# The shift of the entry layer norm in a Mamba and local attention kernel: five small ScalarE instructions in place of one VectorE product of two SBUF operands

## The reference

```
x = x + layernorm(mamba(layernorm(x)))
x = x + layernorm(attention_stack(layernorm(x)))
```

## Time and profile before

| | us |
|---|---|
| median of 3 runs | 2461.28 |
| lowest and highest | 2460.6, 2464.99 |
| the profiled execution, its own time | 2461.61 |
| its span, first to last instruction | 2459.8 |
| mean granted TensorE clock | 0.943 |
| TensorE, VectorE, ScalarE, GpSimd busy | 1893.9, 1892.7, 1778.1, 1711.4 |

### The profile page before, as it was taken

How to read it: one execution, slowest core, us unless ns; L and a number is a source line. 1 busy time by engine, 2 the same in 40 slices (tenths; PEclk the granted TensorE clock), 3 DMA queues, 4 the chain that set the end, 5 groups by cost and what they waited for, 6 DMA issues and landing times.

```text
span 2459.8 us, 44075 instructions
## 1 busy us (share of the span) xinstructions
PE 1893.9 (77%) x15808; PEld 1114.3 (45%) x15936; DVE 1892.7 (77%) x3477; ACT 1778.1 (72%) x3955; POOL 1711.4 (70%) x1540
## 2 busy tenths in 40 slices
PE   2156778797878879797878879697888879787865
PEld 0013345353635445363635445363645545363634
DVE  3557797978879797988878797988879797887442
ACT  2245778696978878696878878696877869685644
POOL 1969595977959596886959596885959597792010
PEclk9977999899999989999999999999999989999988
DMA  4444443535344343534544353534543353531000
GB/s 162 126 120 115 112 105 104 132 83 146 103 130 117 100 121 92 134 86 131 129 129 103 103 124 96 138 87 130 130 115 99 110 127 90 137 99 33 17 20 9
DMA packets 126346, 261.09 MB, mean 106 GB/s; under 512 B 26928, under 2 KB 59696, under 8 KB 125872
## 3 DMA queue, kind: packets, MB, share of 16 engines
q1 hardware_dynamic: 126128, 258.27, 39.6%
HBM read 185.42 MB, written 42.99 MB: 93 GB/s over the span
## 4 chain that ended last, share of the span: by engine, by line
PE 38%; DVE 23%; ACT 13%; issue 9%; POOL 8%; DMA 4%; SPq 0%; DVEq 0%; POOLq 0%; ACTq 0%
DVE hs L618 6%; DVE m L892 4%; PE f_bank L342 4%; PE b_bank L342 4%; DVE kr L906 3%; POOL gy L663 3%; DMA spread<-steps 3%; POOL dbu L646 3%; ACT da L594 3%; PE b_bank L703 3%; PE f_bank L746 3%; PE y_sum L571 2%; DVE b_bank L896 2%; PE b_bank L773 2%; DVE ss L879 2%
## 5 line engine op out<-in xcount | busy, mean ns | idle before, releaser
L618 DVE TENSOR_TENSOR_SCAN hs<-da,dbu 128x512 f32<-128x512 f32 x512 | 622.2, 1215 | 127.1 <-POOL dbu L646 82.0
L663 POOL TENSOR_TENSOR gy<-hs,bc 128x512 f32<-128x512 f32 x512 | 652.1, 1274 | 41.5 <-DVE hs L618 31.2
L646 POOL TENSOR_TENSOR dbu<-spread,bc 128x512 f32<-128x512 f32 x512 | 651.5, 1274 | 9.1 <-DMA spread<-steps 9.0
L594 ACT ACTIVATE da<-spread,rest 128x512 f32<-128x512 f32 x512 | 359.4, 702 | 159.0 <-DVE hs L618 135.1
L703 PE MATMUL b_bank<-rest,h_t 128*128 128x512 f32 x384 | 227.9, 694 | 96.6 <-DVE kr L906 92.5
L960 POOL TENSOR_TENSOR kr<-kr,rn 128x512 f32<-128x512 f32 x256 | 264.8, 1043 | 42.3 <-ACT rn L817 37.0
L703 PE MATMUL f_bank<-rest,h_t 128*128 128x512 f32 x384 | 217.6, 665 | 72.1 <-DVE kr L906 64.2
L571 PE MATMUL y_sum<-gy,rest 128*32 128x512 f32 x1024 | 147.0, 649 | 92.4 <-POOL gy L663 92.3
L342 PE MATMUL f_bank<-first,kr 128*128 128x128 f32 x768 | 128.4, 298 | 78.9 <-DVE kr L906 49.8
L342 PE MATMUL b_bank<-first,kr 128*128 128x128 f32 x768 | 123.7, 296 | 57.8 <-DVE kr L906 41.8
L1106 POOL TENSOR_TENSOR xs<-xs,v 128x512 f32<-128x512 f32 x16 | 18.9, 1183 | 213.3 <-ACT xs L337 213.3
(11 more groups left out here) (168 smaller groups left out, 4748.2 us busy)
## 6 DMA issues: line engine op xcount, KB each, us to landing
spread<-steps SPq DMA_DIRECT2D x256, 512.0 KB, 5.1
vs<-v SPq DMA_DIRECT2D x96, 260.0 KB, 5.9
bc<-bc_rows SPq DMA_DIRECT2D x32, 512.0 KB, 6.2
steps<-k_t SPq DMA_DIRECT2D x32, 512.0 KB, 2.7
gate<-gates SPq DMA_DIRECT2D x32, 512.0 KB, 5.7
gates<-kr SPq DMA_DIRECT2D x16, 512.0 KB, 3.4
gates<-late SPq DMA_DIRECT2D x16, 512.0 KB, 4.3
vs<-v SPq DMA_DIRECT2D x32, 130.0 KB, 4.5
```

Of the source, the lines that this page charges most:

```text
L594: e.activation(da[:, :], spread[:, slot(b, s // 2), 0, :], ACT.Exp, scale=a_neg[:, s:s + 1]).then_inc(decayed.sem, 1)
L618: e.tensor_tensor_scan(hs[:, s % 2, :], da[:, :], dbu[:, s % 2, :], 0.0, ALU.mult, ALU.add).then_inc(scanned.sem, 1)
L646: e.tensor_tensor(dbu[:, s % 2, :], spread[:, slot(b, s // 2), 1, :], bc[:, s % 2, :], ALU.mult).then_inc(fed.sem, 1)
L663: e.tensor_tensor(gy[:, s % 8, :], hs[:, s % 2, :], bc[:, 2 + s % 2, :], ALU.mult).then_inc(read_out.sem, 1)
```

## The change

Four things change.

1. In the entry, VectorE no longer makes the shift. `dve_enter` loses that step.
2. ScalarE makes it instead, in one new step, `act_norm_shift`: a copy of the means with scale -1 into `lv` (128x4), and then four products of 128x1 elements, `lv[:, t] * rs[:, t]`, with `rs` as the scale operand. It waits on itself before the products (`negated`) and before the normalisation (`shifted`). The other layer norms keep L331.
3. Two counters are added, and `n_e` counts two measurements in place of three. `act_normalise` no longer waits for VectorE in the entry.
4. The table `ORDER` is written anew for all engines. Most of it stands as it was. Steps change places with their neighbours in many spots, and at SP some move further.

```diff
 ORDER = {
     "pe": (
-        "A1 B1 A1 B1 A1 B3 A3 B2 A3 B5 A1 B1 A1 B2 A2 B3 A1 B1 A1 M1 B2 A2 B1 M1 A1 B1 A1 B4 A1 B1 A1 B4 A1 B4 A1 "
+        "A1 B1 A1 B1 A2 B1 A1 B2 A1 B2 A1 B2 A1 B1 A1 B2 A2 B2 A1 B3 A1 B1 A1 M1 B1 A1 B2 A2 B1 A1 M1 B1 A1 B4 A1 "
...
     "sp": (
-        "M1 F2 M5 A1 M1 B1 M1 E1 B1 M3 A1 M6 C1 M5 S3 B1"),
+        "M1 F2 M8 B2 M1 E1 M1 A1 M1 A1 M3 C1 M6 S1 M1 B1 S2"),
...
-        n_e, n_y, n_x, n_o = Norm("_enter"), Norm("_y", 2), Norm("_x1"), Norm("_out")
+        n_e, n_y, n_x, n_o = Norm("_enter", 2), Norm("_y", 2), Norm("_x1"), Norm("_out")
...
+        e_negated, e_shifted = sig("e_negated", 1), sig("e_shifted", 1)
...
+        def act_norm_shift(E, e, w, b, negated, shifted):
+            e.activation(w.lv[:, :], w.mv[:, :, 0], ACT.Copy, scale=-1.0).then_inc(negated.sem, 1)
+            E.wait_ge(*negated(b))
+            for t in range(NT):
+                op = e.activation(w.mr[:, t:t + 1], w.lv[:, t:t + 1], ACT.Copy, scale=w.rs[:, t:t + 1])
+            op.then_inc(shifted.sem, 1)
+            yield
+            E.wait_ge(*shifted(b))
+
         def act_normalise(E, e, w, b, dst, src):
-            E.wait_ge(*w.measured(b, 2))
+            if w is not n_e:
+                E.wait_ge(*w.measured(b, 2))
...
             yield from dve_norm_stats(E, e, n_e, b, lambda t: x_in[:, t, :])
-            dve_norm_shift(E, e, n_e, b)
-            yield
...
             yield from act_norm_scale(E, e, n_e, b)
+            E.wait_ge(*n_e.scaled(b, 1))
+            yield from act_norm_shift(E, e, n_e, b, e_negated, e_shifted)
```

More of the change, by code:

```diff
@@ L44 @@
     "pe": (
[3 rows of a table removed]
[3 rows of a table added]
     "act": (
[4 rows of a table removed]
[4 rows of a table added]
     "dve": (
[4 rows of a table removed]
[4 rows of a table added]
     "pool": (
-        "F4 C1 A2 B1 A1 M2 B1 M2 B2 M3 B1 M1 A1 M1 B1 M1 B1 M1 A1 B1 M2 A1 M2 A1 B1 M1 B1 A1 B2 M3 A1 M3 A1 M1 A2 "
-        "M44"),
+        "F4 C1 A2 B1 A1 M1 B1 M3 B3 M3 A1 M4 B2 A1 M2 B1 M1 A1 M1 A1 B1 M1 B1 A1 B2 M3 A1 M3 A1 M1 A2 M44"),
     "sp": (
-        "M1 F2 M5 A1 M1 B1 M1 E1 B1 M3 A1 M6 C1 M5 S3 B1"),
+        "M1 F2 M8 B2 M1 E1 M1 A1 M1 A1 M3 C1 M6 S1 M1 B1 S2"),
 }
```

## The result

The changed kernel takes 2473.5 us in the median of 5 runs (2467.4 to 2478.3), the kernel before 2461.3 in 5 runs beside it. The ratio is 1.0045, with a 95% interval of 1.0025 to 1.0064: slower by 0.45%, some 11 us, where 0.18% less was forecast. It lies outside the range of 2449 to 2466 us. The profiled execution took 2474.06 us.

A forecast was written before the change was run, and what follows sets the result against it. No engine bounds the whole; GpSimd is nearest to it in the stretch of the changed instruction. 2461.6 - 4.3 - 1.2 + 1.0 = 2457.1 us, forecast as 2456.8 against the median; 8-in-10 range 2449 to 2466 us.

The forecast's parts named there:

- The removed instruction: Entry's shift on VectorE: without it GpSimd's 0.33 us wait ahead of read-out 19 goes, 13 times, 4.3 us gained.
- The filling's 1.2 us: Pipeline filling: the second sequence's read-out, 1.23 us late behind a 3.72 us shift, gets that time back.
- Rival 4: Entry: the wait is GpSimd's or the counters' and returns at the next instruction; 2461.1 us, within a shared chance of 0.20.
- The price of the five: ScalarE's five new instructions in the entry: 0.95 to 2.05 us together, taken as 1.2, covered in a steady block.
- the first sequence's normalisation: First sequence, ScalarE: nothing covers the new instructions, 1.2 us replace a 0.23 us wait, so 1.0 us is lost.
- The slower rival: TensorE's entry turn waits 1.0 us a block for ScalarE's normalisation; 2474 us, chance 0.13.
- The moved steps: New order on VectorE, TensorE and SP, including the rotations from 1124 on: counted as nothing.
- bound of 1.2 us a block: Stretch from 1124: VectorE busy 31.8 of 33 us, so the new rotation order could win or lose only 1.2 us.
- the 6.6 us at 1.2 GHz: TensorE in the stretch from 1124: a moved low-clock time could give up to 1.2 us a block either way; taken as zero.
- my two terms for the start: Start of the kernel: 1.2 us gained in the filling, 1.0 us lost in the first sequence.
- The later part and SP: Moved statistics, entry turn, feed-forward output between blocks and SP's loads and copies: each counted as nothing.
- upper end of 0.84 us: VectorE's statistics of the back's feed-forward, moved into idle time: at most 0.84 us a block, counted as nothing.

The follow-up runs named there:

- ops_only: The five ScalarE instructions put into the kernel before, with its old order table; 2455.9 us, ratio 0.9978 to the kernel before.
- drain_before: The changed kernel with the old order table for blocks from 13 on; 2464.2 us, ratio 1.0012 to the kernel before.
- steady_before: The changed kernel with the old order in blocks 0 to 12, new rows only from block 13 on; 2463.0 us, ratio 1.0001 to the kernel before.
- v3_first: The changed kernel with one swap in TensorE's row: back's product v3 ahead of front's v2, as before; 2459.0 us, ratio 0.9977 to the kernel before.
- rot_before: The changed kernel with the old order for each block's first steps on TensorE, ScalarE, VectorE and GpSimd's whole row; 2442.5 us, ratio 0.9929 to the kernel before.
- table_only: The kernel before with the new order table, VectorE still making the shift; 2483.3 us, ratio 1.0093 to the kernel before.
- rot_before_dve_shift: The changed kernel with the old rotation part in all four engine rows and VectorE's shift kept; 2447.4 us, ratio 0.9941 to the kernel before.

## Why the prediction was wrong

- **The removed instruction: right.** The wait for GpSimd left with it, and so did the gap ahead of read-out 19, in the changed kernel and in `ops_only`. I had 4.3 us for it; the exchange alone gave 5.4 in all, 2.7 to 8.4 by its interval. The filling's 1.2 us within the sum were not measured apart. Rival 4 is excluded, as nothing of the wait came back at the next instruction.
- **The price of the five: right,** 1.1 us against 1.2, and the first sequence's normalisation came 1.1 us later against 1.0 (`ops_only` begins it at 10.41; the earlier trace rows at 9.31).
- **The slower rival: the wrong place.** It gave 2474 us and the measurement is 2473.5, but by chance. The entry's turn waits in no steady block. The slower side came from the rotations and from the end.
- **The failed step** is this one, in "The moved steps": "From 1124 on the order of rotations changes on VectorE and TensorE. [...] I take zero." Both the value and its bound failed. With the rotation part put back, the blocks are 1.7 us shorter on average and the whole is 1.16 points shorter. I took the bound of 1.2 us a block from VectorE's idle time in the stretch from 1124. But the rotations go on behind 1157: v2 and v3, whose places were changed, stand at the border of the two stretches, and VectorE misses their results in the second one. There VectorE was busy for 25.3 of 28 us, and that fell to 23.7 in the long blocks. I had read what each engine does in the stretch, and not which instruction stands behind which wait.
- I had named the 6.6 us at 1.2 GHz in that stretch, "after TensorE waited for VectorE", and said that a move of it would count either way. What I didn't do was to lay the moved products on such a wait. The clock of the stretch behind, 0.94 in the same rows, I left out. Four TensorE steps in series behind the wait at v2 take 3.3 us at one clock and 6.3 at the other. v3 back ahead of that wait was worth 14.5 us of the whole.
- **The end** was in no term. I had nothing for the blocks from 13 on, and the new order costs 6 to 8 us there, about half of the loss. Which of its steps does it was not separated.
- **The filling** came out 2.9 us shorter after (the first residual of x1 at 149.1 us instead of 152.0). No cause can be given for it. `drain_before` has the same rows there as the changed kernel and comes to 150.5 us, and `ops_only` and `steady_before`, which are alike there too, to 152.2 and 150.4. So one trace differs from its like by up to 1.8 us, and the net of my two terms for the start, -0.2 us, is far below that.
- **The later part and SP: zero, and that was wrong the other way.** With the old rotation part they give 0.9929 against 0.9978 for the exchange alone, some 12 us of gain. My upper end of 0.84 us for the moved statistics would be 10.9 us over 13 blocks. Which move of the later part brings it was not tried.

What stays open: between `v3_first` (0.9977) and `rot_before` (0.9929) lie another 0.48 points in the rotation rows. The changed kernel's first scan of a block starts 28.1 us after the residual of x1, and so it does in `v3_first`, while it is 27.5 in `rot_before` and 27.4 before. Over 13 blocks that 0.6 us would be 7.8 of some 12 us. No run separates the rest. ScalarE's and GpSimd's rows were not tried alone.

## What to carry to other kernels

When an order table changes, go first to the long waits of an in-order queue and ask which ready instruction has been moved from ahead of a wait to behind it. It can cost its own length on the chain that the wait releases, at the clock that holds there, and it is missed on another engine a stretch later, so that the idle time of the stretch is no bound for it. Whether it does cost depends on the other engines' rows, so try the swap alone. Look at the end of a pipeline as well, where the same rows meet other neighbours. Test an edit and the reordering that comes with it apart: here the edit gained 0.2%, its new order lost 0.9%, and a mix of both orders gained 0.7%.

## What was not expected of the hardware

- A loop of equal blocks can run in two lengths, and the granted clock alternates with them. After the change the blocks were 138.6 and 141.4 us in turn, with 6.6 and 17.3 us at 1.2 GHz. `drain_before`, with the same rows up to block 12, repeats it, `rot_before` has 137.7 and 138.8 in turn, and one swap of two steps of TensorE ended it. Why the low stretch is long in every second block, and whether the clock or the order of waits drives the turn, is not shown.
- A mean granted clock doesn't order kernels by time. The profiled executions are 2442.2 us at 0.931 (`rot_before`), 2461.6 at 0.943 (before) and 2464.5 at 0.949 (`v3_first`). The same kernel, the one before, was granted 0.923 to 0.948 in its executions, and its times of 2456 to 2468 us don't follow that. Much of the spread between the traces is made before the first residual, where TensorE has little to do: the clock there was 0.66 in `rot_before`, 0.68 in the changed kernel, 0.94 before and 1.00 in `v3_first`.
- VectorE's small product with two SBUF operands, which took 3.72 us in the filling, was behind the late read-out after all. The other two kernels with the shift on VectorE, `table_only` and `rot_before_dve_shift`, have a row of 3.72 us as well. With the shift on ScalarE the read-outs of this place start on time, in the changed kernel and in `ops_only`. GpSimd's timeline of the changed kernel:

```profile
106.96 1.26 POOL L673 TENSOR_TENSOR gy<-hs,bc 128x512 f32<-128x512 f32 x1
108.18 1.26 POOL L677 TENSOR_TENSOR y<-y,gate 128x512 f32<-128x512 f32 x1
109.40 1.26 POOL L656 TENSOR_TENSOR dbu<-spread,bc 128x512 f32<-128x512 f32 x1
```

In the "SBUF — State Buffer" page of the Trainium skill ("Who interferes with whom") the later of the two waits for the other to finish. Here the instruction lasted 3.72 us, from 104.88 to 108.60, beside three GpSimd instructions of 1.3 us in a row, the last of which ended at 108.58. So it outlasted all three, and the measurement decides.
